# A recurrent two-layer block on one core: a further order of the second phase's instructions, with two more pairs of chunk transpositions on TensorE

## The chip, the core and the metric

The kernel runs on one core of one Trainium2 chip. The metric is the device time of one execution in microseconds, and the median of several runs is what counts. A core has five engines that work from instruction streams of their own: TensorE (PE; its weight loads are shown apart as PEld), VectorE (DVE), ScalarE (ACT), GpSimd (POOL) and SyncE (SP), which here issues nearly all transfers. They meet only at semaphores.

## The reference, cut to what matters

The input is 16 sequences of 512 tokens of width 128. Two layers follow one another, and each is x + s * silu(f):

```
xn = layernorm(x)
s  = softmax(Q Q^T * scale) Q,          Q = xn Wq + bq            # per sequence of 512
L  = xn phi^T + phi_b                   # 64 experts x 32 slots = 2048 slots per token
D, C = softmax(L, over slots), softmax(L, over experts)
Y  = tanh(layernorm(clip(D^T xn))) expert_w + expert_b            # per slot
x  = x + s * silu(C Y)

xn = layernorm(x)
a  = exp(8 r log sigmoid(lam)),  r = sigmoid(xn W_rg + b_rg),  i = sigmoid(xn W_ig + b_ig)
h_t = a h_(t-1) + sqrt(1 - a^2 + 1e-6) * i * (xn W_in)            # a scan over the 512 tokens
s  = (rmsnorm(h) * norm_w) W_out
f  = sigmoid(xr W_r) * (relu(xk W_k)^2 W_v),  xr, xk = mixes of xn with the token before
x  = x + s * silu(f)
```

## The kernel before, in words

The first phase (up to about 620 us) computes the slot logits, their exponentials and the dispatch of tokens to slots, and stores the exponentials of every token and slot in memory. A short middle part makes the expert outputs (YHI and YLO, a high and a low part). The second phase, where the whole change lies, works on 16 blocks, one sequence of 512 tokens each, in a software pipeline: while block b is combined and its attention scores are made, the attention of block b-1 is finished and the second layer of block b-2 is computed.

What one block asks of each engine in the second phase:

- **The 16 chunks.** A chunk is 128 slots of 512 tokens. POOL weighs two chunks (a group) with the softmax factors (`weigh_exps`, L146) in a ring of four groups, which SP fills (`load_exps`, L153; a load waits until the group that held the ring slot has been transposed). `exps_turned(i, c)` (L1229) transposes a chunk on PE in four transpositions of 128x128 in f32, into one of two banks ct; it waits until DVE has finished with the chunk two before. ACT copies the bank to `chi` (`chunk_high`, L1595), DVE makes the rest `clo` (`chunk_low`, L1927), and `combine(i, c)` (L1239, L1240, L1242) adds three matmuls of 512 columns to the bank yac. After chunk 15, `y_tanh` (ACT, L1587) and `silu_y` (DVE, L1963) read yac.
- **Attention.** `project` (L1245 to L1247 with at<-xn_transposed) makes Q in the bank at0, once `attended` (ACT, L1574) of the block before has emptied it. `query` (ACT, L1544) adds the bias and writes b_qf. `values` (PE, L1261) transposes b_qf in four pieces. `scores(i, r)` (L1275, L1277, L1278) for four row tiles, then `probabilities`, `scaled` (ACT), `turn(i, k)` (PE, L1289, four transpositions), `turn_high`, `turn_low` and `weigh(i, k)` (L1299, L1300, L1302).
- **The second layer.** `mean` (L1311), `variance` (L1319), `decay_gate`, `input_gate`, `input_product` (three matmuls each, L1245 to L1247 with lp<-r_xh), `ffn_k` (L1344), `ffn_r` (L1350), `ffn_v` (L1356), `state_mean` (L1362), `state_out` (L1370). The seven with one name and one line are single matmuls in f32, which the trace shows as two passes of 512 columns. Around them ACT computes `deviation_log` (L1605), `deviation_inverse` (L1610), `decay_tanh` (L1617), `decay` (L1622), `decay_squares` (L1629), `input_log` (L1680), `input_root` and others; DVE `normalise` (L1977), the mixes, the scan and the output.
- **Tables.** Ln and Tanh lie in different table sets of ACT, so `log_table` (L1708) and `tanh_table` (L1712) load one in turn, four loads per block.

The order within each engine is written out by hand as a list of calls in a loop over blocks, each engine having its own, with a list of its own for the last block (LAST); a call outside the range of blocks does nothing. Every helper waits for its inputs and for the readers of the buffer that it overwrites, so that an order changes times but not results. On PE an order can also not overtake itself: a call that waits holds up all that stands behind it.

Of the kernel before, what the change touches and what calls it, by code (L numbers as in the profile page):

```python
# [24 lines left out]
def build(nc, t):  # L25
# [44 lines left out]
    with root:  # L70
# [1050 lines left out]
        with ExitStack() as ph:  # L1121
# [61 lines left out]
            def sync2(e):  # L1183
# [35 lines left out]
            def tensor2(e):  # L1219
# [211 lines left out]
                for i in range(-2, NB + 1):  # L1431
# [52 lines left out]
                    mean(i - 2)  # L1484
                    combine(i - 1, 8)
# [34 lines left out]
                last_decay_gate(1)  # L1520
                last_ffn_r(0)
                last_input_gate(1)
                last_input_product(0)
                ffn_v(LAST - 1)
                last_ffn_k(0)
                state_mean(LAST - 1)
                last_ffn_k(1)
                last_input_product(1)
# [308 lines left out]

# [555 lines left out]
```

## Time and profile before

| what | value |
|---|---|
| median of 3 runs (range) | 1180.55 us (1180.03 to 1183.29) |
| the profiled execution's own time | 1181.29 us |
| its span, first to last instruction | 1179.1 us |
| PE, DVE, ACT, POOL busy | 98%, 87%, 83%, 82% of the span |
| second phase, one block | 35.04 us |
| mean granted TensorE clock | 0.997 |

The span is 2.2 us shorter than the same execution's time, and the median of the runs is 0.7 us below that time. Times in the rows count from the start of the span. In the timeline a row's start and its duration are given; matmuls overlap, so what one costs TensorE is read from its start to the start of the next.

### The profile page before, as it was taken

The numbers are of one execution on the slowest core, as the hardware profiler recorded it, in microseconds if no ns is written. First come the engines' busy times: TensorE is split into PE (matmuls) and PEld (weight loads), VectorE is DVE, ScalarE is ACT, GpSimd is POOL, SyncE is SP. The second block draws the span as 40 slices with busy tenths as digits, with TensorE's granted clock in tenths as the row PEclk, the third lists the DMA queues.
The fourth block names the chain that finished last, engine by engine and source line by source line (L and its number), as shares of the span: only waits on it lengthen the run. The fifth ranks groups of instructions, "written<-read, shape, count | busy, mean of one in ns | idle before, by whom it ended". The sixth has DMA issues, their size and how long they took to land. (4 is left out here: it accounts for less than half of the span.)

```text
span 1179.1 us, 17775 instructions
## 1 busy us (share of the span) xinstructions
PE 1150.5 (98%) x5165; PEld 796.8 (68%) x5165; DVE 1029.6 (87%) x1608; ACT 984.0 (83%) x2128; POOL 964.2 (82%) x770
## 2 busy tenths in 40 slices
PE   7999999999999999999989999999999999999996
PEld 6666666566666666666457777777777777777773
DVE  7999999999999999999766778888877888887877
ACT  5877877777767666667668999999999999999998
POOL 3999999898999999999788878878777878777751
PEclk9999999999999999999999999999999999999999
DMA  4435435434424433443764444344444343444420
GB/s 132 167 137 201 152 130 186 156 123 165 155 110 161 156 125 121 161 156 114 224 206 158 130 141 154 115 135 134 144 138 148 116 151 117 136 144 143 139 76 19
DMA packets 125264, 167.38 MB, mean 142 GB/s; under 512 B 7536, under 2 KB 102000, under 8 KB 125040
## 3 DMA queue, kind: packets, MB, share of 16 engines
q1 hardware_dynamic: 123984, 165.71, 41.4%
q8 instruction: 43, 0.70, 0.2%
q10 hardware_dynamic: 1184, 0.53, 0.2%
q14 instruction: 53, 0.43, 0.1%
HBM read 90.71 MB, written 75.50 MB: 141 GB/s over the span
## 5 line engine op out<-in xcount | busy, mean ns | idle before, releaser
L146 POOL TENSOR_TENSOR exp_slots_loaded<-exp_slots_loaded,slot_max 128x1024 f32<-128x1024 f32 x128 | 330.5, 2599 | 9.9 <-DMA exp_slots_loaded<-exp_slots 9.3
L868 POOL TENSOR_TENSOR dd<-ed,rz 128x512 f32<-128x512 f32 x256 | 267.6, 1051 | 24.4 <-ACT rz L698 23.2
L573 PE MATMUL acc<-dd,xns 128*128 128x512 f32 x512 | 261.1, 592 | 0.7 <-POOL dd L868 0.7
L1927 DVE TENSOR_TENSOR clo<-ct,chi 128x512 fp32r<-128x512 f32 x256 | 170.1, 680 | 31.9 <-ACT chi L1595 30.9
L176 POOL TENSOR_TENSOR ch<-exp_slots_loaded 128x512 f32<-128x512 f32 x128 | 165.9, 1296 | 30.6 <-ACT exp_slots_loaded L676 29.6
L805 DVE TENSOR_REDUCE mr<-lg 128x16 fp32r<-128x512 f32 x256 | 168.2, 686 | 18.3 <-PE lg L514 15.9
L667 ACT ACTIVATE ed<-lg 128x512 f32<-128x512 f32 x256 | 145.7, 594 | 39.7 <-PE lg L550 37.8
L676 ACT ACTIVATE exp_slots_loaded<-lg 128x512 f32<-128x512 f32 x256 | 145.4, 594 | 25.7 <-PE lg L559 23.8
L821 DVE TENSOR_REDUCE zd<-ed 128x32 f32<-128x1024 f32 x128 | 154.7, 1209 | 1.5 <-ACT ed L667 1.5
L814 DVE TENSOR_REDUCE mr<-lg 128x32 fp32r<-128x1024 f32 x128 | 155.6, 1216 | 0.0
L1595 ACT ACTIVATE chi<-ct 128x512 fp32r<-128x512 f32 x256 | 147.5, 597 | 7.5 <-PE ct L1229 5.2
L1229 PE MATMUL ct<-identity,exp_slots_loaded 128*128 128x128 f32 x1024 | 143.5, 273 | 3.1 <-DVE clo L1927 2.3
L559 PE MATMUL lg<-shift_experts_to_slots,mt 128*128 128x512 f32 x256 | 144.8, 595 | 1.1 <-ACT ed L667 1.1
L512 PE MATMUL lg<-phi_then_expert_out,xn_transposed 128*128 128x512 f32 x256 | 140.0, 547 | 0.5 <-DVE xn_transposed L421 0.5
L1229 PEld LDWEIGHTS ct<-identity,exp_slots_loaded 128*128 128x128 f32 x1024 | 121.3, 141 | 27.2 <-issue 7.1
L1239 PE MATMUL yac<-chi,phi_then_expert_out 128*128 128x512 f32 x256 | 126.0, 492 | 0.3 <-ACT chi L1595 0.3
L573 PEld LDWEIGHTS acc<-dd,xns 128*128 128x128 f32 x512 | 95.6, 192 | 22.1 <-issue 3.8
L1242 PE MATMUL yac<-clo,phi_then_expert_out 128*128 128x512 f32 x256 | 102.4, 400 | 0.0
L514 PE MATMUL lg<-phi_then_expert_out,xn_transposed 128*128 128x512 f32 x256 | 101.8, 398 | 0.0
L1240 PE MATMUL yac<-chi,phi_then_expert_out 128*128 128x512 f32 x256 | 101.5, 397 | 0.0
L513 PE MATMUL lg<-phi_then_expert_out,xn_transposed 128*128 128x512 f32 x256 | 101.2, 395 | 0.0
L559 PEld LDWEIGHTS lg<-shift_experts_to_slots,mt 128*128 128x128 f32 x256 | 48.0, 188 | 78.0 <-ACT ed L667 62.9
(317 smaller groups left out, 2506.2 us busy)
## 6 DMA issues: line engine op xcount, KB each, us to landing
exp_slots<-exp_slots_loaded SPq DMA_DIRECT2D x128, 512.0 KB, 3.4
exp_slots_loaded<-exp_slots SPq DMA_DIRECT2D x128, 512.0 KB, 3.5
xns<-xn_rows SPq DMA_DIRECT2D x128, 64.0 KB, 1.9
b_xraw<-in_xT SPq DMA_DIRECT2D x16, 256.0 KB, 3.6
out_t<-b_ti SPq DMA_DIRECT2D x15, 256.0 KB, 2.0
expert_w_late<-in_expert_w SPq DMA_DIRECT2D x5, 512.0 KB, 11.4
xn_rows<-slot_sum SPq DMA_DIRECT2D x8, 256.0 KB, 2.5
expert_w_early<-in_expert_w SPq DMA_DIRECT2D x3, 512.0 KB, 5.8
```

What stands on the lines that cost most here:

```text
L146: e.tensor_tensor(rows, rows, joined(SM, b)[:, h].unsqueeze(2).broadcast_to([P, TPB, GC * EPC, NP]), ALU.mult).then_inc(s_we)
L176: e.tensor_tensor(ch[v % 2][:, :], ec[v % RE][:, 0:BANK], ec[v % RE][:, BANK:HS], ALU.add).then_inc(s_ch)
L559: e.matmul(lg[v % 2][:, bank(k)], mt[v % 2][:, :], S2M[:, bank(k)], start=False, stop=True, skip_group_check=True).then_inc(s_s2)
L573: e.matmul(acc[k][:, :], xns[v % RX][:, :], dd[v % RX][:, bank(k)], start=tile == 0, stop=tile == NT - 1, skip_group_check=True).then_inc( ...
L667: e.activation(ed[v % RD][:, bank(k)], lg[v % 2][:, bank(k)], ACT.Exp).then_inc(s_ed)
L805: e.tensor_reduce(mr[v % 2][:, k * HN // 2:(k + 1) * HN // 2], lg[v % 2][:, bank(k)].rearrange("q (n p) -> q n p", p=NP), AX_X, ALU.max).t ...
L814: e.tensor_reduce(mr[v % 2][:, HN:G], lg[v % 2][:, :].rearrange("q (n p) -> q p n", p=NP), AX_X, ALU.max).then_inc(s_mx)
L821: e.tensor_reduce(zd[v % 2][:, :], ed[v % RD][:, :].rearrange("q (n p) -> q n p", p=NP), AX_X, ALU.add).then_inc(s_zd)
L868: e.tensor_tensor(dd[v % RX][:, bank(k)].rearrange("q (n p) -> q n p", p=NP), ed[v % RD][:, bank(k)].rearrange("q (n p) -> q n p", p=NP), ...
L1229: done = e.transpose(ct[c % 2][:, rows(k)], ECL[:, g // GC % RL, k, c % GC * P:(c % GC + 1) * P], IDENT[:, :])
L1595: e.activation(chi[g % RC][:, :], ct[c % 2][:, :], ACT.Copy).then_inc(c_h)
L1927: e.tensor_tensor(clo[g % RC][:, :], ct[c % 2][:, :], hi_f32(chi[g % RC][:, :]), ALU.subtract).then_inc(c_l)
```

## The change

Nothing is added or removed: each engine issues the same instructions with the same waits in another order, in the loop of the second phase and in its written-out end. On PE the chunks 5 and 6 and the chunks 7 and 8 are each transposed in one go where each stood alone (6 and 8) or beside other work (5, 7); the chunks 2 and 3 stand directly ahead of `values`. `input_gate`, `input_product` and `ffn_k` change places, `ffn_r`, `scores(3)`, `state_out` and `mean` move. The diff, cut: the loops of PE, ACT and DVE in full where they differ, the ends to what the prediction speaks of.

```diff
     for i in range(-2, NB + 3):
+        exps(i + 1, 2)
         load_x(i)
-        exps(i + 1, 2)
...
@@ -1445,44 +1445,44 @@
         exps_turned(i - 1, 0)
         decay_gate(i - 3)
         weigh(i - 2, 1)
-        combine(i - 2, 14)
         turn(i - 2, 3)
         exps_turned(i - 1, 1)
+        combine(i - 2, 14)
         combine(i - 2, 15)
         weigh(i - 2, 2)
         weigh(i - 2, 3)
-        input_gate(i - 3)
+        input_product(i - 3)
+        ffn_k(i - 3)
+        project(i - 1)
+        combine(i - 1, 0)
         exps_turned(i - 1, 2)
         exps_turned(i - 1, 3)
-        project(i - 1)
-        combine(i - 1, 0)
+        values(i - 1)
+        input_gate(i - 3)
         combine(i - 1, 1)
-        ffn_k(i - 3)
-        input_product(i - 3)
-        values(i - 1)
         exps_turned(i - 1, 4)
         scores(i - 1, 0)
+        ffn_r(i - 3)
         combine(i - 1, 2)
         scores(i - 1, 1)
         exps_turned(i - 1, 5)
+        exps_turned(i - 1, 6)
+        scores(i - 1, 2)
         combine(i - 1, 3)
-        ffn_r(i - 3)
-        scores(i - 1, 2)
-        exps_turned(i - 1, 6)
         combine(i - 1, 4)
         ffn_v(i - 3)
+        scores(i - 1, 3)
+        combine(i - 1, 5)
         exps_turned(i - 1, 7)
-        combine(i - 1, 5)
+        exps_turned(i - 1, 8)
         combine(i - 1, 6)
-        exps_turned(i - 1, 8)
-        scores(i - 1, 3)
         state_mean(i - 3)
-        state_out(i - 3)
         combine(i - 1, 7)
         exps_turned(i - 1, 9)
         exps_turned(i - 1, 10)
+        state_out(i - 3)
+        combine(i - 1, 8)
         mean(i - 2)
-        combine(i - 1, 8)
         combine(i - 1, 9)
         exps_turned(i - 1, 11)
...
     combine(LAST, 10)
-    combine(LAST, 11)
     exps_turned(LAST, 13)
     turn(LAST, 1)
     exps_turned(LAST, 14)
+    combine(LAST, 11)
     weigh(LAST, 0)
     combine(LAST, 12)
     turn(LAST, 2)
+    exps_turned(LAST, 15)
     weigh(LAST, 1)
     combine(LAST, 13)
-    exps_turned(LAST, 15)
+    turn(LAST, 3)
     decay_gate(LAST - 1)
-    turn(LAST, 3)
     combine(LAST, 14)
     combine(LAST, 15)
     weigh(LAST, 2)
...
-    last_ffn_r(1)
     state_out(LAST - 1)
     last_ffn_v(1)
+    last_state_mean(0)
     last_state_out(0)
-    last_state_mean(0)
+    last_state_mean(1)
     last_state_out(1)
-    last_state_mean(1)
...
     for i in range(-2, NB):
         chunk_high(i - 1, 4)
+        ffn_r_tanh(i - 3)
         probabilities(i - 1, 0)
         next_factors(i)
         chunk_high(i - 1, 5)
         probabilities(i - 1, 1)
-        ffn_r_tanh(i - 3)
         scaled(i - 1, 0)
-        state_squares(i - 3)
         chunk_high(i - 1, 6)
         scaled(i - 1, 1)
-        chunk_high(i - 1, 7)
+        state_squares(i - 3)
         probabilities(i - 1, 2)
         ffn_tanh(i - 3)
+        chunk_high(i - 1, 7)
         chunk_high(i - 1, 8)
         log_table(i - 1)
+        scaled(i - 1, 2)
+        chunk_high(i - 1, 9)
         state_log(i - 3)
-        scaled(i - 1, 2)
+        probabilities(i - 1, 3)
         state_inverse(i - 3)
-        chunk_high(i - 1, 9)
-        probabilities(i - 1, 3)
         chunk_high(i - 1, 10)
         scaled(i - 1, 3)
         squares(i - 2)
...
         turn_high(i - 1, 1)
         chunk_high(i - 1, 13)
         chunk_high(i - 1, 14)
+        scaled_r(i - 2)
+        turn_high(i - 1, 2)
         scaled_k(i - 2)
-        turn_high(i - 1, 2)
-        scaled_r(i - 2)
         chunk_high(i - 1, 15)
         chunk_high(i, 0)
         decay_tanh(i - 2)
         decay(i - 2)
+        turn_high(i - 1, 3)
         decay_squares(i - 2)
-        turn_high(i - 1, 3)
         chunk_high(i, 1)
         y_tanh(i - 1)
         log_table(i - 1)
...
         query(i)
         chunk_high(i, 2)
         chunk_high(i, 3)
+        ffn_k_relu(i - 2)
         input_tanh(i - 2)
-        ffn_k_relu(i - 2)
         value_high(i)
         input_root(i - 2)
         ffn_k_squares(i - 2)
...
     y_tanh(LAST)
+    log_table(LAST)
     decay_squares(LAST - 1)
-    log_table(LAST)
     ffn_k_relu(LAST - 1)
     last_squares(0)
-    input_log(LAST - 1)
+    ffn_k_squares(LAST - 1)
     last_deviation_log(0)
     last_squares(1)
     last_deviation_inverse(0)
+    input_log(LAST - 1)
+    last_deviation_log(1)
+    tanh_table(LAST)
+    last_deviation_inverse(1)
+    input_tanh(LAST - 1)
     input_root(LAST - 1)
-    last_deviation_log(1)
-    last_deviation_inverse(1)
-    tanh_table(LAST)
-    input_tanh(LAST - 1)
-    ffn_k_squares(LAST - 1)
...
+    log_table(LAST)
     state_squares(LAST - 1)
-    log_table(LAST)
...
+    ffn_tanh(LAST - 1)
     state_inverse(LAST - 1)
-    ffn_tanh(LAST - 1)
-    last_state_squares(0)
     last_ffn_tanh(0)
     last_ffn_tanh(1)
+    last_state_squares(0)
...
     for i in range(-2, NB):
+        chunk_low(i - 1, 8)
         ffn_silu(i - 3)
-        chunk_low(i - 1, 8)
         row_max(i - 1, 3)
         chunk_low(i - 1, 9)
         weights(i - 1, 3)
+        chunk_low(i - 1, 10)
         state_normalised(i - 3)
-        chunk_low(i - 1, 10)
-        gate_second(i - 3)
         chunk_low(i - 1, 11)
         turn_low(i - 1, 0)
         chunk_low(i - 1, 12)
+        gate_second(i - 3)
         output(i - 3)
         normalise(i - 2)
         turn_low(i - 1, 1)
         normalised_split(i - 2)
         chunk_low(i - 1, 13)
         chunk_low(i - 1, 14)
-        mix_k(i - 2)
         turn_low(i - 1, 2)
         chunk_low(i - 1, 15)
+        turn_low(i - 1, 3)
         chunk_low(i, 0)
-        mix_r(i - 2)
-        turn_low(i - 1, 3)
-        chunk_low(i, 1)
+        mix_k(i - 2)
         next_max(i + 1)
         one_minus(i - 2)
         silu_y(i - 1)
+        mix_r(i - 2)
+        chunk_low(i, 1)
         residual(i - 1)
         project_split(i)
         chunk_low(i, 2)
...
         scan_input(i - 2)
+        chunk_low(i, 4)
         row_max(i, 1)
         weights(i, 0)
-        chunk_low(i, 4)
         scan(i - 2)
+        weights(i, 1)
         chunk_low(i, 5)
-        weights(i, 1)
         row_max(i, 2)
         chunk_low(i, 6)
         ffn(i - 2)
         next_inverse(i + 1)
+        chunk_low(i, 7)
         weights(i, 2)
-        chunk_low(i, 7)
...
     for i in range(-2, NB):
         next_shifts(i + 2)
+        gate_attended(i)
         if i < 0:
             exps_weighed(i + 1, 2)
-        gate_attended(i)
         query_low(i + 1)
```

Left out are further moves of one to three places in the written-out end of PE, ACT and DVE. In the loop of ACT the calls not shown keep their place: `chunk_high(i - 1, 11)`, `turn_high(i - 1, 0)`, `chunk_high(i - 1, 12)`, `deviation_log`, `tanh_table`, `deviation_inverse`, and later, behind `log_table`, `attended(i - 1)`, `input_log(i - 2)` and `tanh_table`.

## Rows read from the trace of the kernel before

**Rows 1.** The page: engines' busy time, share of the span, instructions; issue to landing of a load.

```profile
PE 1150.5 (98%) x5165; PEld 796.8 (68%) x5165; DVE 1029.6 (87%) x1608; ACT 984.0 (83%) x2128; POOL 964.2 (82%) x770
...
exp_slots_loaded<-exp_slots SPq DMA_DIRECT2D x128, 512.0 KB, 3.5
```

**Rows 2.** Busy time by stretch: one block of the loop, and the end.

```profile
core 0: us, PE busy (x) PEld busy (x) DVE busy (x) ACT busy (x) POOL busy (x), PEclk, DMA share, GB/s
892.21:927.25 35.04, 35.04 (x185) 26.88 (x184) 28.82 (x51) 34.43 (x61) 27.82 (x16) 1.00 0.43 136
...
1151.07:1179.10 28.03, 18.19 (x68) 10.45 (x66) 20.85 (x48) 23.55 (x46) 3.28 (x4) 0.94 0.06 20
```

**Rows 3.** The source line of mean: its matmuls, first and last start.

```profile
L1311 PE MATMUL lp<-b_x,weights x30: 592/594/595, 646.8 to 1137.9; 128*128 128x512 f32 x30
```

**Rows 4.** Timeline of PE, 896 to 904 us: start, duration, engine, line, operation.

```profile
900.52 0.40 PE L1242 MATMUL yac<-clo,phi_then_expert_out 128*128 128x512 f32 x1
900.86 0.66 PE L1289 MATMUL at<-identity,b_e 128*128 128x128 f32 x4
901.27 0.48 PE L1239 MATMUL yac<-chi,phi_then_expert_out 128*128 128x512 f32 x1
...
901.83 0.48 PE L1242 MATMUL yac<-clo,phi_then_expert_out 128*128 128x512 f32 x1
902.14 1.04 PE L1229 MATMUL ct<-identity,exp_slots_loaded 128*128 128x128 f32 x8
902.93 0.48 PE L1245 MATMUL lp<-r_xh,weights_high 128*128 128x512 f32 x1
903.25 0.39 PE L1246 MATMUL lp<-r_xl,weights_high 128*128 128x512 f32 x1
```

**Rows 5.** Timeline of ACT and DVE, from the variance to the second turn.

```profile
896.86 0.69 ACT L1605 ACTIVATE b_ty<-lp,epsilons 128x512 f32<-128x512 f32 x1 [0.16 <-PE lp L1319]
...
899.52 0.69 DVE L1977 TENSOR_TENSOR xn<-lp,b_ty 128x512 f32<-128x512 f32 x1 [1.13 <-ACT b_ty L1610]
900.13 0.68 DVE L1958 TENSOR_TENSOR ptl<-at,pth 128x512 fp32r<-128x512 f32 x1
```

**Rows 6.** Timeline of PE, from combine 15 to values, and chunk 7.

```profile
906.45 0.39 PE L1242 MATMUL yac<-clo,phi_then_expert_out 128*128 128x512 f32 x1
...
908.76 1.03 PE L1229 MATMUL ct<-identity,exp_slots_loaded 128*128 128x128 f32 x8
...
911.73 1.02 PE L1344 MATMUL lp<-b_xk,weights 128*128 128x512 f32 x2
912.19 0.79 PE L1245 MATMUL lp<-r_xh,weights_high 128*128 128x512 f32 x1
912.82 0.39 PE L1246 MATMUL lp<-r_xl,weights_high 128*128 128x512 f32 x1
...
913.28 0.60 PE L1261 MATMUL at<-identity,b_qf 128*128 128x128 f32 x4
...
920.97 0.60 PE L1229 MATMUL ct<-identity,exp_slots_loaded 128*128 128x128 f32 x4
```

**Rows 7.** Timeline of ACT, 902 to 912 us.

```profile
902.05 0.80 ACT L1636 ACTIVATE b_xr<-xn,epsilons,vectors 128x512 f32<-128x512 f32 x1
902.78 1.09 ACT L1595 ACTIVATE chi<-ct 128x512 fp32r<-128x512 f32 x2
...
904.63 0.82 ACT L1622 ACTIVATE b_aa<-b_aa,derived_vectors 128x512 f32<-128x512 f32 x1
905.48 0.63 ACT L1629 ACTIVATE b_a<-b_aa 128x512 f32<-128x512 f32 x1
...
906.97 0.60 ACT L1587 ACTIVATE b_ty<-yac 128x512 f32<-128x512 f32 x1
...
911.41 0.69 ACT L1544 ACTIVATE b_qf<-at,vectors 128x512 f32<-128x512 f32 x1
```

**Rows 8.** Timeline of POOL: the weighing of two groups, the later for chunk 14.

```profile
925.32 4.73 POOL L146 TENSOR_TENSOR exp_slots_loaded<-exp_slots_loaded,slot_max 128x1024 f32<-128x1024 f32 x2
```

More of the change, by code:

```diff
@@ L1520, in tensor2 @@
                 last_decay_gate(1)
+                last_input_gate(1)
                 last_ffn_r(0)
-                last_input_gate(1)
+                last_ffn_k(0)
                 last_input_product(0)
                 ffn_v(LAST - 1)
-                last_ffn_k(0)
+                last_input_product(1)
+                last_ffn_k(1)
                 state_mean(LAST - 1)
-                last_ffn_k(1)
-                last_input_product(1)
+                last_ffn_r(1)
                 last_ffn_v(0)
-                last_ffn_r(1)
                 state_out(LAST - 1)
                 last_ffn_v(1)
+                last_state_mean(0)
                 last_state_out(0)
-                last_state_mean(0)
+                last_state_mean(1)
                 last_state_out(1)
-                last_state_mean(1)
             def scalar2(e):
@@ L1835, in scalar2 @@
                     ffn_k_squares(i - 2)
+                chunk_high(LAST, 4)
+                ffn_r_tanh(LAST - 2)
                 probabilities(LAST, 0)
-                chunk_high(LAST, 4)
+                probabilities(LAST, 1)
                 chunk_high(LAST, 5)
-                ffn_r_tanh(LAST - 2)
                 scaled(LAST, 0)
-                probabilities(LAST, 1)
                 chunk_high(LAST, 6)
@@ L1848, in scalar2 @@
                 chunk_high(LAST, 7)
+                chunk_high(LAST, 8)
                 ffn_tanh(LAST - 2)
-                chunk_high(LAST, 8)
                 log_table(LAST)
                 scaled(LAST, 2)
+                chunk_high(LAST, 9)
+                chunk_high(LAST, 10)
                 probabilities(LAST, 3)
-                chunk_high(LAST, 9)
+                state_log(LAST - 2)
                 scaled(LAST, 3)
-                chunk_high(LAST, 10)
-                state_log(LAST - 2)
                 squares(LAST - 1)
-                state_inverse(LAST - 2)
                 chunk_high(LAST, 11)
@@ L1862, in scalar2 @@
                 chunk_high(LAST, 12)
+                state_inverse(LAST - 2)
                 deviation_log(LAST - 1)
+                chunk_high(LAST, 13)
                 deviation_inverse(LAST - 1)
-                chunk_high(LAST, 13)
                 turn_high(LAST, 1)
+                tanh_table(LAST)
                 chunk_high(LAST, 14)
-                tanh_table(LAST)
                 turn_high(LAST, 2)
+                chunk_high(LAST, 15)
                 scaled_r(LAST - 1)
                 scaled_k(LAST - 1)
-                chunk_high(LAST, 15)
+                turn_high(LAST, 3)
                 decay_tanh(LAST - 1)
-                turn_high(LAST, 3)
                 decay(LAST - 1)
                 y_tanh(LAST)
+                log_table(LAST)
                 decay_squares(LAST - 1)
-                log_table(LAST)
                 ffn_k_relu(LAST - 1)
                 last_squares(0)
-                input_log(LAST - 1)
+                ffn_k_squares(LAST - 1)
                 last_deviation_log(0)
@@ L1896, in scalar2 @@
                 last_decay_tanh(1)
+                last_input_tanh(1)
+                last_decay(1)
                 last_ffn_r_tanh(0)
-                last_decay(1)
-                last_input_tanh(1)
                 last_decay_squares(1)
+                log_table(LAST)
                 state_squares(LAST - 1)
-                log_table(LAST)
                 last_input_log(0)
@@ L2207, in vector2 @@
                     next_inverse(i + 1)
+                    chunk_low(i, 7)
                     weights(i, 2)
-                    chunk_low(i, 7)
                 chunk_low(LAST, 8)
+                ffn_silu(LAST - 2)
                 row_max(LAST, 3)
+                chunk_low(LAST, 9)
+                chunk_low(LAST, 10)
                 weights(LAST, 3)
-                chunk_low(LAST, 9)
-                ffn_silu(LAST - 2)
-                chunk_low(LAST, 10)
-                state_normalised(LAST - 2)
                 chunk_low(LAST, 11)
@@ L2221, in vector2 @@
                 chunk_low(LAST, 12)
+                state_normalised(LAST - 2)
+                chunk_low(LAST, 13)
                 gate_second(LAST - 2)
+                turn_low(LAST, 1)
                 normalise(LAST - 1)
-                turn_low(LAST, 1)
                 normalised_split(LAST - 1)
-                output(LAST - 2)
-                chunk_low(LAST, 13)
                 turn_low(LAST, 2)
                 chunk_low(LAST, 14)
-                mix_k(LAST - 1)
+                output(LAST - 2)
+                mix_r(LAST - 1)
                 chunk_low(LAST, 15)
                 turn_low(LAST, 3)
+                mix_k(LAST - 1)
                 silu_y(LAST)
@@ L2236, in vector2 @@
                 last_gate(1)
+                last_residual(1)
                 one_minus(LAST - 1)
[L2238 to L2239 removed]
                 last_normalise(0)
                 last_split(0)
+                last_scaled_k(0)
                 last_low(0)
                 last_normalise(1)
[L2244 removed]
                 gated(LAST - 1)
@@ L2247, in vector2 @@
                 last_low(1)
+                last_mix_k(0)
                 last_mix_r(0)
+                last_scaled_k(1)
+                last_one_minus(0)
                 scan_input(LAST - 1)
-                last_mix_k(0)
+                last_mix_k(1)
                 scan(LAST - 1)
-                last_one_minus(0)
-                last_scaled_k(1)
-                last_mix_k(1)
+                last_one_minus(1)
+                last_mix_r(1)
                 last_ffn_k_relu(0)
-                last_one_minus(1)
                 last_gated(0)
+                ffn(LAST - 1)
                 last_ffn_k_relu(1)
-                last_mix_r(1)
-                ffn(LAST - 1)
+                last_scan_input(0)
                 last_gated(1)
-                last_scan_input(0)
+                last_ffn(0)
                 last_scan_input(1)
-                last_ffn(0)
                 last_scan(0)
@@ L2267, in vector2 @@
                 last_scan(1)
+                ffn_silu(LAST - 1)
                 state_normalised(LAST - 1)
-                ffn_silu(LAST - 1)
+                last_ffn_silu(0)
                 gate_second(LAST - 1)
-                last_ffn_silu(0)
+                last_ffn_silu(1)
                 output(LAST - 1)
-                last_ffn_silu(1)
                 last_state_normalised(0)
```

7 lines of the change are left out of this document (2 added, 5 removed).

## The prediction

> **What bounds the kernel now.** I read the page first, then the busy time by stretch, then the timelines of PE and ACT through one block. On the page PE is busy for 98% of the span, far ahead of DVE, ACT and POOL [rows 1]. The busy time of one block says more: of 35.04 us PE is busy for all 35.04 and ACT for 34.43 [rows 2]. Both are full, and ACT has 0.61 us to spare per block. The granted clock there is 1.00, the 2.4 GHz level. Matmuls overlap, so "busy" hides small holes; I read those from start to start. The first and last start of mean lie 490.9 us apart over 15 blocks, 14 periods of 35.06 us [rows 3], so what a block gains or loses counts 14 times.
>
> The intervals that build a block: a matmul of the three-part kind takes 0.23 us to the next start; eight transpositions take 0.79 to the next start and the matmul behind them 0.32 in place of 0.23, so 0.88 for eight and 0.44 for four [rows 4]; an f32 matmul of two passes takes 0.46 to the next start, and the one behind it 0.63 in place of 0.23, so 0.86 [rows 6]. A block has 84 of the first, 21 groups of four transpositions and seven of the last: 19.5 + 9.2 + 6.0 = 34.7 us, and with under 0.01 for each of 15 borders between the kinds 34.8. The remaining 0.24 us are two holes. The second turn starts 0.34 after the matmul ahead of it in place of 0.23, and its four transpositions last 0.41 to the next matmul in place of 0.35 (0.79 less 0.44); chunk 15 starts 0.31 after its matmul in place of 0.23 [rows 4]. Together 0.11 + 0.06 + 0.08, about 0.24 us. So 14 x 0.24 = 3.4 us is all that an order can win in the loop.
>
> Who makes these holes? ACT waits 0.16 us for the variance; log, table load and inverse follow; DVE waits 1.13 us for them, normalises from 899.52, and turn_low(1) runs from 900.13 to 900.81 [rows 5]; the turn starts at 900.86. The latency from DVE to PE is thus about 0.05 us.
>
> **The change part by part.**
>
> *Longer groups of transpositions.* One group of four costs 0.44 us whether it stands alone or in eight, as what the shorter interval (0.35) gives is taken by the matmul behind (0.32 for 0.23) [rows 4]. What is left per border is under 0.01 us. And counting the unbroken stretches of f32 work (transpositions and two-pass matmuls together) in the loop gives 15 before and 15 after: 5 with 6 and 7 with 8 are joined, but ffn_k, ffn_v, state_mean and mean then stand elsewhere. I take 0. Bounds: the 0.09 us by which the matmul behind a group is longer, won once for each of the two joined pairs and fully (14 x 0.18 = 2.5 us), and nothing.
>
> *The existing holes.* From variance to chunk 15 the loops of PE and ACT are unchanged. DVE has gate_second and output ahead of normalise; it had 1.13 us idle there, the added gate_second takes about 0.9, so normalise keeps its start, by 0.2 us. The two holes stay: 0.
>
> *Moving turn_high(3) ahead of decay_squares on ACT.* decay_squares reads decay, and starts 0.85 us after it [rows 7]; with a copy between, the pair goes at the rate of independent work of that length (0.73) [rows 7]. ACT wins about 0.1 us, but y_tanh must wait for combine 15, whose last matmul starts at 906.45 and ends at 906.84 [rows 6]. The calls ahead of it are the same set, so that stays. y_tanh can start at 906.88 in place of 906.97: 0.09 us earlier.
>
> *values moved forward.* This is the term that decides. On PE, from the last matmul of combine 15 at 906.45: 0.23, then weigh 2 and 3 (1.39) and one three-part product (0.70) reach 908.76, where today the eight transpositions of chunks 2 and 3 start [rows 6]. In the new order ffn_k and project take 0.46 + 0.63 + 0.46 = 1.55 (910.31), combine 0 takes 0.70 (911.01), chunks 2 and 3 0.87: values stands ready at 911.88. It stands at 913.28 now [rows 6]. It reads b_qf, which query writes, and query cannot follow: from y_tanh through two table loads, attended and input_log it is pure ACT work in unchanged order, 4.44 us (906.97 to 911.41), then 0.69 for query itself [rows 7]. So 906.88 + 4.44 + 0.69 = 912.01, and with 0.05 of latency values starts at 912.06. That is 0.18 us late, plus the 0.06 that four transpositions take longer behind a wait: 0.23 us per block. Behind the waiting call on PE stand input_gate, combine 1, chunk 4 and all else; ACT waits for input_gate, and DVE for scores. Block 1 is free of it (ACT has no decay of a block before), blocks 2 to 15 are not: 14 x 0.23 = **3.3 us**. Bounds: nothing, if ACT is 0.2 us sooner, and 0.35 us per block (4.9 us) if the wait also keeps project from loading weights during ffn_k.
>
> *Does ACT have room for it?* With input_gate, ffn_r and chunk 5 later, ACT waits in my table of starts about 0.12 us at input_tanh, 0.13 at ffn_r_tanh, 0.35 at chunk 5, and 0.21 at chunk 7, which PE transposes 1.6 us later than 920.97 [rows 6]: 0.81 us. It has 0.61 idle [rows 2], 0.23 from the longer block and 0.1 won, 0.94. So it fits, by 0.13 us. Combines 5 to 9 find their copies over 1 us early, so these waits of ACT stay off PE. Cost 0.
>
> *What moves past queues.* SP issues the load of group 2 ahead of load_x: load_x then waits up to 0.5 us for chunk 13, and its block is needed 11 us later. The ring slots of groups 1 and 3 come free later, by 2.3 and 1.6 us. A load lands 3.5 us after issue [rows 1], so group 7 is there near 926.7, and POOL takes it as the second of the two from 925.32, near 927.7 [rows 8]; 1 us of cover. If that is gone, chunk 14 pays one for one. Chunk 6, transposed 1.1 us earlier, finds its group weighed 1.3 us before. Cost 0. On DVE chunk_low(1) is later by 3 us, and chunk 3 needs it only 0.2 to 0.3 us after it is done; a delay there would be swallowed by the wait at values.
>
> *The end.* From y_tanh of the last block to the end take 28.03 us, in which ACT is busy for 23.55 with five table loads [rows 2]. The new order has as many loads, and one load each goes ahead of decay_squares, of an inverse and of state_squares. The same interval rule (a dependent successor costs 0.85, an independent one 0.73) [rows 7] gives ACT 0.15 us. The scan of block 14 comes 0.8 us later but ahead of the state squares behind the load. I take -0.15 us; bounds -1 and +1.5, the latter about a table load that lands on the chain.
>
> The sum: 3.3 - 0.15 = +3.1 us. Against the profiled execution that is 1181.29 + 3.1 = 1184.4 with a span of 1182.2; its own time lies 0.74 above the median, so against the median **1183.6 us**.
>
> **The rivals.**
>
> A, the forecast: values waits for query in 14 blocks. Own range 1182 to 1185.5. Chance 0.53.
>
> B, no net difference: ACT comes early enough at query, or my starts on PE are 0.2 us off, and both old holes stay. For it: 0.2 us is small against sums over a dozen calls. 1180.5, chance 0.25.
>
> C, slower, ACT becomes the bound: the place is chunk 5, which ACT copies behind ffn_r_tanh, and which is now transposed behind ffn_r. It decides from the point where the waits of ACT pass its room, 0.13 us above my sum. If chunks 5 and 7 come 0.3 us later each, a block grows by 0.4 us further: 14 x 0.4 = 5.6 on top, 1189. Chance 0.13.
>
> D, faster: the holes close, since each new slack lets chunk 13 or the inverse come sooner, or the joined groups pay 0.09 each; 1180.5 - 3.4 = 1177.1. Against it: the chain of rows 5 hangs on the variance alone. Chance 0.08.
>
> E, the clock falls in the long groups of transpositions. The granted clock is 1.00 in a block that already has twelve in a row [rows 2]. At the 1.2 GHz level twelve would take 1.3 us more, 14 x 1.3 = 18 us, 1199. Chance 0.01. The Trainium skill, page "TensorE: Matmul & The Clock Gate", Part 4, PE-mode transpose, says that transposing does not count as busy for the clock and does not bring the full one. By that rule this change would be the wrong way; the trace does not agree, as its 84 transpositions per block leave the clock at 1.00.
>
> The change may also not do what it is called for, in the sense that no border goes away; that is already in A and B, where the grouping is worth nothing.
>
> **How the numbers follow.** The forecast is A's 1183.6. About 0.3% (3.5 us) is what a measurement of this kernel can tell from no change, so the borders are 1177.0 and 1184.1. Faster: D, 0.08. Slower: C and E, 0.14, and the upper part of A, 0.21: 0.35. Same: 0.57. The range 1178.6 to 1187.5 takes in A and B with their bounds and leaves out most of D, two thirds of C, and E.
>
> **What would show it.** In the trace of the changed kernel a block should take 35.26 us by the starts of mean; PE should have a new hole at values (L1261), released by ACT's query (L1544), with 0.2 us before it; the holes at the second turn and at chunk 15 should be there as now; four transpositions should still cost 0.44; ACT should wait for PE at chunks 5 and 7, and its busy time stay near 34.3. I am wrong on the main term if values starts with no wait, on the room of ACT if combine or turn wait for ACT on PE, and on the grouping if the block is under 35.0 us.

## The result and the profile after

| | before | after |
|---|---|---|
| median of 20 runs (range) | 1180.88 us (1179.32 to 1183.29) | 1182.68 us (1181.52 to 1184.20) |
| ratio, 95% interval | | 1.0015 (1.0008 to 1.0022) |
| the profiled execution: time, span, granted clock | 1181.29, 1179.1, 0.997 | 1182.97, 1180.9, 0.996 |

The changed kernel is slower by 0.15%, 1.8 us. By the bound of 0.3% that the prediction set this counts as no change, though the interval leaves out 1; it lies 0.9 us under the forecast of 1183.6. I read the same views in the same order as before. First the busy time of one block (mean to mean) and of the end; the columns are those of [rows 2].

```profile
893.60:928.78 35.18, 35.16 (x183) 26.99 (x182) 28.21 (x51) 34.33 (x61) 26.79 (x16) 1.00 0.43 135
...
1152.73:1180.90 28.17, 18.31 (x68) 10.88 (x66) 21.27 (x47) 23.33 (x46) 3.07 (x4) 0.91 0.08 27
```

The block is 35.18 us long in place of 35.04, at the same clock, and ACT is busy for 34.33 us of it in place of 34.43. To sum over all blocks I take the source line of variance, which stands at the same place of PE's loop in both kernels (mean itself was moved). The rows give its first and last start, before and after:

```profile
L1319 PE MATMUL lp<-b_ty,ones_over_width x30: 592/594/595, 650.5 to 1141.5; 128*128 128x512 f32 x30
```

```profile
L1319 PE MATMUL lp<-b_ty,ones_over_width x30: 592/594/595, 650.1 to 1143.2; 128*128 128x512 f32 x30
```

The distance goes from 491.0 to 493.1 us, +2.1. What lies ahead of it is 0.4 shorter, and what lies behind it goes from 37.6 to 37.7. Together that is the 1.8 us between the two spans. So the loss is in the loop, and the loop should have one new hole. PE around the two old holes, then from combine 15 to values (timeline; start, duration):

```profile
901.20 0.39 PE L1242 MATMUL yac<-clo,phi_then_expert_out 128*128 128x512 f32 x1
901.54 0.66 PE L1289 MATMUL at<-identity,b_e 128*128 128x128 f32 x4
901.95 0.48 PE L1239 MATMUL yac<-chi,phi_then_expert_out 128*128 128x512 f32 x1
...
907.10 0.40 PE L1242 MATMUL yac<-clo,phi_then_expert_out 128*128 128x512 f32 x1
...
909.41 1.02 PE L1344 MATMUL lp<-b_xk,weights 128*128 128x512 f32 x2
910.10 0.56 PE L1245 MATMUL at<-xn_transposed,weights_high 128*128 128x512 f32 x1
910.50 0.40 PE L1246 MATMUL at<-xn_transposed,weights_high 128*128 128x512 f32 x1
...
911.65 1.03 PE L1229 MATMUL ct<-identity,exp_slots_loaded 128*128 128x128 f32 x8
912.71 0.65 PE L1261 MATMUL at<-identity,b_qf 128*128 128x128 f32 x4
913.12 0.48 PE L1245 MATMUL lp<-r_xh,weights_high 128*128 128x512 f32 x1
```

The second turn still starts 0.34 after the matmul ahead of it and lasts 0.41 to the next, as in [rows 4]. The new hole is at 912.71: behind the eight transpositions at 911.65 values could have started 0.88 later, at 912.53. It starts 0.18 later than that, and lasts 0.41 in place of 0.35 to the next matmul. So the new hole is 0.18 + 0.06 us per block, the two terms of the forecast. (That eight transpositions take 0.88 is seen where nothing waits behind them, with values late below.) Who releases it stands in the source line of values:

```profile
L1261 PE MATMUL at<-identity,b_qf x64: 272/273/330, 604.6 to 1124.2; 128*128 128x128 f32 x64
its engine sat idle before it (us, times) until:
  ACT b_qf L1544: 3.5, 14
```

Fourteen waits, all on query, 3.5 us in sum, 0.25 us each. ACT's side, y_tanh and query, then chunk 5 and the pair of copies that begins with chunk 7 (timeline of ACT):

```profile
907.53 0.60 ACT L1587 ACTIVATE b_ty<-yac 128x512 f32<-128x512 f32 x1
...
911.97 0.69 ACT L1544 ACTIVATE b_qf<-at,vectors 128x512 f32<-128x512 f32 x1
...
918.62 0.60 ACT L1595 ACTIVATE chi<-ct 128x512 fp32r<-128x512 f32 x1 [0.25 <-PE ct L1229]
...
923.85 1.08 ACT L1595 ACTIVATE chi<-ct 128x512 fp32r<-128x512 f32 x2 [0.24 <-PE ct L1229]
```

y_tanh starts 0.43 after the last matmul of combine 15 (907.53 less 907.10), query ends 5.13 after y_tanh starts (4.44 + 0.69), and values starts 0.05 later. ACT waits for PE at chunks 5 and 7, about 0.25 us each. From start to start no matmul of PE is late for the copies of chunks 5 to 9.

### The profile page after: what moved, and what is told of

Its sections match the earlier page's. It is cut to its first block and busy times, and to the rows that moved or that the text cites. A ratio compares the mean times of both kernels' runs of the same rounds, so it can differ in the third digit from the quotient of the medians.

```text
span 1180.9 us, 17775 instructions
## 1 busy us (share of the span) xinstructions
PE 1153.2 (98%) x5165; PEld 798.5 (68%) x5165; DVE 1015.6 (86%) x1608; ACT 982.3 (83%) x2128; POOL 949.3 (80%) x770
## 5 line engine op out<-in xcount | busy, mean ns | idle before, releaser
L146 POOL TENSOR_TENSOR exp_slots_loaded<-exp_slots_loaded,slot_max 128x1024 f32<-128x1024 f32 x128 | 311.6, 2455 | 5.4 <-DMA exp_slots_loaded<-exp_slots 4.6
L1229 PE MATMUL ct<-identity,exp_slots_loaded 128*128 128x128 f32 x1024 | 138.1, 272 | 1.3 <-PEq L1112 0.8
L1239 PE MATMUL yac<-chi,phi_then_expert_out 128*128 128x512 f32 x256 | 134.6, 526 | 0.3 <-ACT chi L1595 0.3
L1240 PE MATMUL yac<-chi,phi_then_expert_out 128*128 128x512 f32 x256 | 101.4, 396 | 0.0
```

The costliest lines, as they stand in the source:

```text
L146: e.tensor_tensor(rows, rows, joined(SM, b)[:, h].unsqueeze(2).broadcast_to([P, TPB, GC * EPC, NP]), ALU.mult).then_inc(s_we)
L1229: done = e.transpose(ct[c % 2][:, rows(k)], ECL[:, g // GC % RL, k, c % GC * P:(c % GC + 1) * P], IDENT[:, :])
L1239: e.matmul(yac[:, :], YHI[:, c, :], chi[g % RC][:, :], start=c == 0, stop=False)
L1240: e.matmul(yac[:, :], YLO[:, c, :], chi[g % RC][:, :], start=False, stop=False)
```

## The experiments

Each kernel is given with the distance from first to last start of the line of variance (491.0 us before, 493.1 after), which holds 14 blocks. Values late, values early alone, pairs split and holes closed ran beside the kernel before at 1180.53 us, the other four beside it at 1180.63; beside the changed kernel it had 1180.88. So a difference between medians of two experiments can be off by 0.3 us, and the distance in the loop is the better measure.

**values late** (after, one call moved). Is the new wait all that the change costs, or would ACT, now full, hold the block at its length?

```diff
-                    values(i - 1)
                     input_gate(i - 3)
+                    values(i - 1)
                     combine(i - 1, 1)
```

> The changed kernel with values(i - 1) and input_gate(i - 3) exchanged in the loop of PE, so that values stands 0.70 us later. Theory W (the loss is the wait of values for query, 0.18 us, and 0.055 for the four transpositions behind a wait, in 14 blocks): the wait goes, a block takes 35.19 - 0.24 = 34.95 us, and the median falls by 3.3 us from 1182.7 to 1179.4, which is 1.5 below the kernel before. Theory R (ACT is what bounds the new order, seen in its waits of 0.25 us each ahead of chunks 5 and 7): the block stays at 35.19 and the time at 1182.7. Theory G (the longer groups of transpositions cost the time): 1182.7 too.

Measured: 1179.23 us (1178.74 to 1180.69), ratio to before 0.9988 (0.9979 to 0.9997); distance 649.0 to 1139.1, 490.1 us. PE's timeline at values and the matmul behind it:

```profile
910.75 0.60 PE L1261 MATMUL at<-identity,b_qf 128*128 128x128 f32 x4
911.10 0.48 PE L1239 MATMUL yac<-chi,phi_then_expert_out 128*128 128x512 f32 x1
```

The eight transpositions of chunks 2 and 3, with nothing waiting behind them:

```profile
909.17 1.03 PE L1229 MATMUL ct<-identity,exp_slots_loaded 128*128 128x128 f32 x8
909.96 0.48 PE L1245 MATMUL lp<-r_xh,weights_high 128*128 128x512 f32 x1
```

The trace has no wait of values any more, and values lasts 0.35 again. The medians differ by 1182.68 - 1179.23 = 3.45 us for one call. Set against the kernel before beside which each ran, it is 3.1 (+1.8 and -1.3), and in the loop 3.0 (493.1 - 490.1). The forecast was 3.3: the wait is the cost, and ACT does not bind. The same distances show something else. Without the wait the loop is 0.9 us shorter than that of the kernel before, so the rest of the change is worth a little, and the 2.1 us of the loop are 3.0 lost at values and 0.9 won elsewhere. This order beats both kernels, the old one by 1.3 us.

**values early alone** (the kernel before, values moved ahead of ffn_k and input_product): the same cost, larger, without the rest of the change.

```diff
+                    values(i - 1)
                     ffn_k(i - 3)
                     input_product(i - 3)
-                    values(i - 1)
```

> The kernel before with one call moved: values(i - 1) straight behind combine(i - 1, 1), ahead of ffn_k and input_product. PE reaches it at 911.73 us in the block of the trace of before, and query ends at 912.10, so with 0.05 of latency it starts at 912.15. Theory W: a hole of 0.42 us and 0.055 behind it, 0.475 per block in 14 blocks, 6.6 us slower: 1187.5 against 1180.9. Were PE able to pass over a waiting transposition, or were such a wait taken out of the two old holes, the time would be that of before.

Measured: 1187.14 us (1185.73 to 1188.57), ratio 1.0053 (1.0041 to 1.0065); distance 648.8 to 1146.0, 497.2 us. The source line of values:

```profile
L1261 PE MATMUL at<-identity,b_qf x64: 272/273/330, 605.2 to 1126.9; 128*128 128x128 f32 x64
...
  ACT b_qf L1544: 12.9, 28
```

This line counts two waits per block, that of the weight load and that of the matmul, which overlap. From start to start values comes 0.63 us after the matmul ahead of it (913.01 to 913.64) in place of 0.23, and its transpositions last 0.06 longer: 0.46 per block against the 0.475 expected. Of +6.6 us the loop shows 6.2. How far a call is moved ahead of its input prices the move, in either kernel.

**pairs split** (after): is grouping worth anything by itself? Three pairs of chunks are taken apart: 5 from 6 and 7 from 8, which the change had joined, and 9 from 10, which stood together before it too.

```diff
-                    exps_turned(i - 1, 6)
                     scores(i - 1, 2)
+                    exps_turned(i - 1, 6)
...
-                    exps_turned(i - 1, 8)
                     combine(i - 1, 6)
+                    exps_turned(i - 1, 8)
...
+                    combine(i - 1, 8)
                     exps_turned(i - 1, 10)
                     state_out(i - 3)
-                    combine(i - 1, 8)
```

> The changed kernel with three pairs of chunks taken apart on PE: scores(2) between chunks 5 and 6, combine(6) between 7 and 8, combine(8) between 9 and 10. Two more borders between the kinds of matmul per block. Theory W, with a border worth 0.004 us: 2 x 0.004 x 14 = 0.1 us, so 1182.8, within 1 us if chunks 6 and 8, each 0.7 us later, wake no new wait. Theory G plus (a joined pair wins the 0.09 us by which the matmul behind it is longer): 14 x 3 x 0.09 = 3.8 us slower, 1186.5. Theory G minus (long groups cost time): faster, under 1181.

Measured: 1201.65 us (1201.12 to 1202.26), ratio 1.0177 (1.0164 to 1.0190); distance 651.7 to 1161.9, 510.2 us. All three theories missed, by 15 us and more. One of three moves had to be costly for a reason of its own, and the next kernels take them apart.

**two pairs split** (after; 5 from 6 and 9 from 10, while 7 and 8 stay together: the first and the third edit above).

> The changed kernel with only two of the pairs apart: scores(2) between chunks 5 and 6, combine(8) between 9 and 10; 7 and 8 stay together. If a border between the kinds of matmul is worth 0.004 us and nothing else hangs on it, 14 x 2 x 0.004 = 0.1 us: 1182.8. If a joined pair wins 0.09 us, 14 x 2 x 0.09 = 2.5 us slower, 1185.2. If the 20 us that three pairs apart cost have to do with pairs as such, two thirds of it, 1195.

Measured: 1183.18 us (1182.30 to 1184.49), ratio 1.0021 (1.0012 to 1.0030); distance 649.5 to 1142.7, 493.2 us, against 493.1 with the pairs joined. PE around chunks 5 and 6:

```profile
917.46 0.60 PE L1229 MATMUL ct<-identity,exp_slots_loaded 128*128 128x128 f32 x4
917.81 0.48 PE L1275 MATMUL at<-r_qh 128*128 128x512 f32 x1
918.13 0.39 PE L1277 MATMUL at<-r_ql,r_qh 128*128 128x512 f32 x1
```

Four transpositions take 0.35 and the matmul behind them 0.32. Eight take 0.79 and 0.32 (values late, 909.17), so 0.44 for four either way. The loop is the same to 0.1 us and the intervals of the two ratios overlap: longer groups are worth nothing, as far as these two pairs show. The third pair, 7 and 8, can't be tried so, as the next kernel shows.

**7 from 8 split** (after, one call: the second edit above).

> The changed kernel with combine(6) between chunks 7 and 8 and nothing else, one call moved. In the trace with three pairs apart chunk 8 comes 0.7 us later, chunk_low(8) on DVE behind it, and ffn_silu (two inputs in SBUF) then starts 0.3 us after POOL has begun to weigh a group and lasts 2.64 us in place of 0.75; row_max(3), probabilities(3), scaled(3) and the first turn are late behind it. Theory P (this collision): the whole loss again, 36.5 us per block, 1201 to 1202. Theory B (borders and pairs): a third of it or less, under 1190.

Measured: 1201.44 us (1200.88 to 1203.76), ratio 1.018 (1.0166 to 1.0194); distance 653.8 to 1163.7, 509.9 us. This one call makes 18.8 of the 19.0 us. The chain in one block, ACT first, then DVE, POOL, ACT and PE, in rows of their timelines:

```profile
937.73 0.60 ACT L1595 ACTIVATE chi<-ct 128x512 fp32r<-128x512 f32 x1 [0.54 <-PE ct L1229]
...
938.36 0.69 DVE L1927 TENSOR_TENSOR clo<-ct,chi 128x512 fp32r<-128x512 f32 x1 [0.37 <-ACT chi L1595]
938.97 2.61 DVE L2016 SCALAR_TENSOR_TENSOR b_f<-b_xr,b_kr 128x512 f32<-128x512 f32 x1
941.50 0.68 DVE L1939 TENSOR_REDUCE nmx<-at 128x1 f32<-128x512 f32 x1
...
938.65 2.38 POOL L146 TENSOR_TENSOR exp_slots_loaded<-exp_slots_loaded,slot_max 128x1024 f32<-128x1024 f32 x1
...
942.40 0.69 ACT L1559 ACTIVATE b_e<-at,nmx 128x512 f32<-128x512 f32 x1 [0.88 <-DVE nmx L1943]
...
944.94 0.33 PE L1289 MATMUL at<-identity,b_e 128*128 128x128 f32 x1 [0.65 <-ACT b_e L1579]
```

Chunk 8 stands 0.7 us later on PE, so ACT waits 0.54 for it and DVE 0.37 for ACT. That moves ffn_silu (L2016) from just before POOL's weighing to just behind its start, where it takes 2.61 us in place of 0.75. The row maximum of the last row tile is late by that, its probabilities wait 0.88, and the first turn waits for the scaled rows on PE. From start to start, a block is 1.28 us longer than in the changed kernel: 0.88 at the first turn, 0.28 ahead of it, where the third matmul of a combine and the chunk behind it start late, and 0.12 at the second turn.

**silu first** (the last kernel, and ffn_silu ahead of chunk_low(8) on DVE): takes the collision away and leaves chunk 8 late.

```diff
-                    chunk_low(i - 1, 8)
                     ffn_silu(i - 3)
+                    chunk_low(i - 1, 8)
```

> The kernel with only the pair 7 and 8 apart, and besides ffn_silu(i - 3) ahead of chunk_low(i - 1, 8) on DVE in the loop, as the kernel before has it. Chunk 8 is as late as in the one with the pair apart, but ffn_silu no longer waits for it and starts before POOL begins the next group. Theory P: ffn_silu lasts about 0.8 to 1.1 us and the loss is gone but for what chunk 8 itself, 0.7 us later, costs: 1183 to 1185. If chunk 8's own lateness is what costs (through its combine, or ACT), it stays near 1201.

Measured: 1187.56 us (1186.63 to 1188.61), ratio 1.0059 (1.0047 to 1.0072); distance 650.2 to 1147.1, 496.9 us. DVE and ACT:

```profile
927.26 0.67 DVE L2016 SCALAR_TENSOR_TENSOR b_f<-b_xr,b_kr 128x512 f32<-128x512 f32 x1
...
927.08 0.60 ACT L1595 ACTIVATE chi<-ct 128x512 fp32r<-128x512 f32 x1 [0.54 <-PE ct L1229]
```

The collision is gone and with it 13.9 of the 18.8 us. The kernel is still 2.6 us above the upper end of what was expected, as 4.9 us remain, 3.8 of them in the loop. ACT still waits 0.54 at chunk 8, and a full ACT can't make that up. Read from start to start on PE, a block is 0.28 us longer than in the changed kernel, in two places. The first turn (L1289 at 932.88) lasts 0.59 to the next start in place of 0.44, so 0.15. The hole at the second turn grows by 0.13: here ACT reaches the variance after PE has it ready, where in the changed kernel it waits for it.

**holes closed** (after): can the two old holes be won with values late? Calls that PE waits for go first on ACT and DVE.

```diff
 # PE
-                    decay_gate(i - 3)
                     weigh(i - 2, 1)
+                    decay_gate(i - 3)
...
-                    values(i - 1)
                     input_gate(i - 3)
                     combine(i - 1, 1)
+                    values(i - 1)
 # ACT
-                    deviation_inverse(i - 2)
                     turn_high(i - 1, 1)
+                    deviation_inverse(i - 2)
 # DVE
-                    normalise(i - 2)
                     turn_low(i - 1, 1)
-                    normalised_split(i - 2)
+                    normalise(i - 2)
                     chunk_low(i - 1, 13)
+                    normalised_split(i - 2)
```

> The changed kernel with values behind combine(i - 1, 1), weigh(i - 2, 1) ahead of decay_gate(i - 3) on PE, turn_high(i - 1, 1) ahead of deviation_inverse(i - 2) on ACT, and turn_low(i - 1, 1) ahead of normalise, chunk_low(i - 1, 13) ahead of normalised_split on DVE. It is to close both old holes (0.22 us per block at the second turn and at chunk 15) besides the one at values. Theory W with PE as the only bound: 34.95 - 0.22 = 34.73 us per block, 1182.7 - 14 x 0.46 = 1176.2. Theory R: ACT, which gets decay_gate 0.5 us later, becomes the bound, and the block stays above 34.95, time 1179.4 or more.

Measured: 1187.16 us (1186.01 to 1191.57), ratio 1.0058 (1.0044 to 1.0073); distance 650.0 to 1147.6, 497.6 us. ACT's decay_tanh and attended, then PE's project:

```profile
907.36 0.69 ACT L1617 ACTIVATE b_aa<-lp,derived_vectors 128x512 f32<-128x512 f32 x1 [0.69 <-PE lp L1247]
...
912.19 0.60 ACT L1574 ACTIVATE b_st<-at 128x512 f32<-128x512 f32 x1
...
911.51 1.03 PE L1344 MATMUL lp<-b_xk,weights 128*128 128x512 f32 x2
912.84 0.50 PE L1245 MATMUL at<-xn_transposed,weights_high 128*128 128x512 f32 x1 [0.29 <-ACT b_st L1574]
```

Both old holes close, and a larger one opens. With decay_gate behind weigh(1), decay_tanh waits 0.69 us, everything to attended is late by that, and project starts 1.33 after ffn_k in place of 0.69. That costs 0.56 us per block, as the matmul behind project's first gives only a part back; two chunks on PE that start late cost 0.2 more. Theory R had named the cause, decay_gate that comes late to ACT, but not its size, and the call on which it lands, project, was not foreseen.

**first hole closed** (values late, and only the pair deviation_inverse and turn_high(1) on ACT, normalise and turn_low(1) on DVE swapped as above).

> The kernel with values behind input_gate, and besides turn_high(i - 1, 1) ahead of deviation_inverse(i - 2) on ACT and turn_low(i - 1, 1) ahead of normalise(i - 2) on DVE. The hole at the second turn (0.15 us) goes; combine 13 then stands 0.15 us earlier and its chunk_low(13) only 0.06, so the hole at chunk 15 grows by 0.09. Net 0.06 per block: 34.90 us and 1179.2 - 0.8 = 1178.4. If ACT were the bound, no gain, 1179.2; if decay_gate waits for the low part that POOL makes later, slower, 1180 or more.

Measured: 1180.94 us (1180.20 to 1182.57), ratio 1.0005 (0.9996 to 1.0013); distance 649.2 to 1140.7, 491.5 us, 1.4 more than with values late alone. DVE, then PE:

```profile
899.13 0.68 DVE L1977 TENSOR_TENSOR xn<-lp,b_ty 128x512 f32<-128x512 f32 x1
...
900.19 1.28 DVE L1927 TENSOR_TENSOR clo<-ct,chi 128x512 fp32r<-128x512 f32 x2
...
900.48 0.40 PE L1240 MATMUL yac<-chi,phi_then_expert_out 128*128 128x512 f32 x1
900.93 0.50 PE L1242 MATMUL yac<-clo,phi_then_expert_out 128*128 128x512 f32 x1
901.27 1.03 PE L1229 MATMUL ct<-identity,exp_slots_loaded 128*128 128x128 f32 x8
```

The turn no longer waits. But chunk_low(13) is a call later in DVE's chain, and the matmul that reads it starts 0.45 after the one ahead, in place of 0.23, and chunk 15 0.34 after that. The hole has moved by one call and grown. The expected gain missed; the time lies where it was expected for a decay_gate that waits, but in this trace decay_gate follows the transpositions without a wait.

## Why the prediction was right

The forecast was +3.1 us, and +1.8 was measured. The stated range also held the time of rival B (no difference), so the time alone decides little; what follows goes by the traces and by the kernels in which the calls were moved.

**values waits for query: right, and the deciding term.** In the frame of the block after (combine 15's last matmul at 907.10 for 906.45, so 0.65 on each start) the forecast was y_tanh at 907.53, values ready at 912.53, query's end at 912.66 and values' start at 912.71. The trace shows 907.53, 912.53, 912.66 and 912.71. The hole is 0.18 + 0.06 us. Moving values back took 3.0 us out of the loop (forecast 3.3), and moving it earlier in the old kernel added 6.6 us. The bound that project also pays did not occur, but only just: project does wait for ACT, as it starts at 910.10, 0.05 after attended is over (910.05), and so 0.69 after ffn_k in place of 0.46. The next matmul follows after 0.40 and not 0.63 [rows 6], so the sum is the same 1.09. The kernel with holes closed shows what a later attended costs.

**Rival B fell**, as the wait at values is there; it would have given the 1180.5 of the kernel before. **Grouping: right, nothing.** Taking 5 from 6 and 9 from 10 apart changed the loop by 0.1 us, where 0.09 us for each would have been 2.5. For 7 and 8 it is carried over, not tried by itself. So the bound did not occur, and with it one half of rival D falls. The other half, that the old holes close, falls by the trace, which has both. Two orders meant to close them moved the hole instead: to project, and to chunk_low(13). Whether another order closes them was not tried. (D's own 1177.1 lies just inside the borders 1177.0 and 1184.1 that the prediction draws for no change, so its chance was counted on the wrong side.)

**The old holes stay: right in mechanism, a little off in size.** The holes at the second turn and at chunk 15 are both there, each within 0.02 us of what it was. The loop gained 2.1 us where the new hole alone gives 3.3. So everything but values, forecast as 0, measured -1.2 us by this sum, and -0.9 by the kernel with values late, which is this term by itself. Per block some 0.02 us are in the hole at the second turn and about 0.01 in an interval at a scores call; the rest lies in intervals that are a few ns shorter each, and its cause stays open. A block takes 35.18 us where the prediction's sign was 35.26; this term is the difference.

**ACT's room: right for this order, with a thin margin.** No matmul of PE is late for ACT's copies, and values late gave nearly all of the forecast 3.3 us back. All four forecast waits (0.12, 0.13, 0.35, 0.21) are in the trace. Those at chunks 5 and 7 are the 0.25 and 0.24 that its rows name. The two others are too short to be named there, but stand in the starts:

```profile
913.51 0.61 ACT L1664 ACTIVATE b_kr<-lp 128x512 f32<-128x512 f32 x1
914.10 0.69 ACT L1650 ACTIVATE b_ti<-lp,derived_vectors 128x512 f32<-128x512 f32 x1
```

input_tanh (L1650) starts 0.59 us behind its neighbour, where with values late, and so with input_gate long done, it starts 0.48 behind: 0.11 us. At ffn_r_tanh it is 0.59 too (916.20 to 916.79), 0.11 over the 0.48 with values late. Rival C's mechanism, that a late chunk makes a full ACT the bound, is real: chunk 8 later by 0.7 us costs 3.8 us in the loop even without the collision. In the changed kernel it stays under that point; by how much was not measured.

**The end: the term was right, and a fall of the clock took the gain back.** -0.15 was forecast; the stretch from y_tanh grew from 28.03 to 28.17 us [rows 2]. ACT's part came as forecast: the first instruction behind the last table load (L1774) starts 21.84 us after y_tanh (1174.57 less 1152.73), where it had been 22.00. Behind it stands one wait of ACT, for the state's mean on PE (L1424), 0.48 us before and 0.72 after. That mean, and the busy time around it (columns of [rows 2]), before and then after:

```profile
1173.90 0.70 PE L1424 MATMUL at<-b_st,ones_over_width 128*128 128x256 f32 x2 [1.57 <-ACT b_st L1770]
1173.80:1174.70 0.90, 0.70 (x2) 0.30 (x2) 0.90 (x3) 0.42 (x3) 0.00 (x0) 1.00 0.03 9
```

```profile
1175.40 0.93 PE L1424 MATMUL at<-b_st,ones_over_width 128*128 128x256 f32 x2 [0.96 <-ACT b_st L1770]
1175.30:1177.20 1.90, 1.78 (x4) 0.95 (x4) 1.83 (x5) 1.15 (x4) 0.00 (x0) 0.61 0.16 60
```

The same two passes last 0.93 us in place of 0.70, and the granted clock of the stretch is 0.61 in place of 1.00. From 1176.00 on it is 0.50, the 1.2 GHz level, and it fell after PE had stood idle for 1.74 and then for 0.96 us. That is the 0.24 us. Values late and two pairs split have the same end as the changed kernel, with the two means on PE as far apart; in their traces the clock stays at 1.00 through the mean, and the wait is 0.49 us. From y_tanh to the instruction behind the wait they take 23.43 and 23.42 us, the changed kernel 23.64, the kernel before 23.57. So with the clock up the new end gains about 0.15 us, as forecast. Of the eight profiled executions with this end the clock had fallen by the mean in four. What sets the moment at which it falls was not tried.

**The clock: rival E fell.** The granted clock of the block is 1.00, with eight and twelve transpositions in a row, as before. This does not decide on the rule for transpositions that the prediction quotes, as the prediction took it to: of a block's 35 us they make 9.2, and the rest are other matmuls. It shows that this mix keeps the full clock.

**What I did not foresee** lies beside the change: an order one call away from it costs 19 us. The prediction compared starts on PE and ACT to 0.05 us, but did not look at what stands side by side on DVE and POOL. The changed kernel is on the good side of this edge, and not by much. The source line of ffn_silu in the kernel before, and then in the kernel after (min/median/max in ns):

```profile
L2016 DVE SCALAR_TENSOR_TENSOR b_f<-b_xr,b_kr x15: 681/1083/1091, 678.5 to 1171.7; 128x512 f32<-128x512 f32 x15
```

```profile
L2016 DVE SCALAR_TENSOR_TENSOR b_f<-b_xr,b_kr x15: 667/757/782, 679.4 to 1172.9; 128x512 f32<-128x512 f32 x15
```

Its median is 2610 ns with 7 and 8 split and 673 with silu first. A start 0.5 us later, as chunk 8's lateness makes it, turns 757 into 2610.

## What to carry to other kernels

Where an engine is full, a new order of its calls is worth the waits that it makes or removes: take the start that PE would reach and the end of the input on the engine that makes it, each summed from the rows of the old trace. Here that gave both to within 0.05 us. Putting work of one kind together was worth nothing here; a row that shows a price per border should come before it is tried. An engine that is nearly full can take its inputs later only as far as its idle time reaches. And look at which DVE operation stands beside the start of a POOL operation before a call is moved by more than a few tenths of a us.

## What was unexpected of the hardware

**DVE held by POOL for a whole instruction.** In the kernel with 7 and 8 split ffn_silu starts at 938.97, 0.32 us after POOL's weighing, and ends at 941.58, 0.55 after POOL's 2.38 us are over (941.03). In the kernel before it starts within POOL's second weighing and ends 0.55 after that too (924.77 against 924.22), so it took 1.08. Rows of POOL and DVE, before:

```profile
918.55 5.67 POOL L146 TENSOR_TENSOR exp_slots_loaded<-exp_slots_loaded,slot_max 128x1024 f32<-128x1024 f32 x2
...
923.69 1.08 DVE L2016 SCALAR_TENSOR_TENSOR b_f<-b_xr,b_kr 128x512 f32<-128x512 f32 x1
```

In the changed kernel it starts at 925.74, 0.15 us ahead of POOL's next weighing, and takes 0.75:

```profile
925.74 0.75 DVE L2016 SCALAR_TENSOR_TENSOR b_f<-b_xr,b_kr 128x512 f32<-128x512 f32 x1
...
925.89 5.19 POOL L146 TENSOR_TENSOR exp_slots_loaded<-exp_slots_loaded,slot_max 128x1024 f32<-128x1024 f32 x2
```

POOL pays as well: these two weighings last 5.19 us where two that follow one another take 4.73 [rows 8].

The Trainium skill, page "SBUF — State Buffer", section "Who interferes with whom", says that a DVE instruction with two SBUF inputs contends with a GpSimd instruction that reads SBUF, for a port pair that works as an exclusive lock; that the first to issue holds it for its whole instruction it says of DVE's 2-port modes. The trace agrees with the first, and shows the second for this operation of two inputs too: three starts, 0.32 us behind, within, and 0.15 us ahead of POOL's, gave 2.61, 1.08 and 0.75 us.

**What a wait costs depends on what stands there.** Four transpositions behind a wait last 0.41 us to the next start and not 0.35 (values after, against values late). A matmul of 512 columns behind a two-pass one, whose start was 0.23 late, gave it all back in its own interval (0.40 for 0.63, project). It did so only there: in the kernel with the first hole closed a matmul of 512 columns behind one of its own kind starts 0.22 late, and the next start is as far behind it as ever, or farther (0.34). So one and the same lateness can cost more than its length, or nothing, by what stands there. Why the transpositions pay was not tried.
